# Two batches at a time, as 4x3 blocks of 256x342: 20 products in place of 2x2 blocks with 7

## The reference

```python
w = weights[conditions]                         # 128 x 128 per batch, picked by an index
x = x + einsum('bct,bcd->bdt', x, w)            # first layer, along the channels
H = einsum('btd,od->bto', x, W)                 # second layer, along the time; W is 1024 x 1024
delta = einsum('btr,bor->bto', einsum('btd,brd->btr', x, A[idx]), Bm[idx]) * scalings[idx]
x = x + H + delta                               # rank 16 adapters, picked by another index
```

## Time and profile before

| | |
|---|---|
| median of the runs | 791.12 us |
| span of the profiled execution, first to last instruction | 788.0 us |
| PE busy | 776.1 us, 98% of the span |
| PEld busy | 720.9 us |
| DVE busy | 529.8 us, 67% |
| ACT busy | 385.6 us, 49% |
| POOL busy | 120.2 us, 15% |
| DMA, mean over the span | 117 GB/s |

### The profile page before, as it was taken

How to read it: one execution, slowest core, us unless ns; L and a number is a source line. 1 busy time by engine, 2 the same in 40 slices (tenths; PEclk the granted TensorE clock), 3 DMA queues, 4 the chain that set the end, 5 groups by cost and what they waited for, 6 DMA issues and landing times.

```text
span 788.0 us, 16267 instructions
## 1 busy us (share of the span) xinstructions
PE 776.1 (98%) x5234; PEld 720.9 (91%) x5234; DVE 529.8 (67%) x942; ACT 385.6 (49%) x722; POOL 120.2 (15%) x283
## 2 busy tenths in 40 slices
PE   6999999999999999999999999999999999999998
PEld 6898999999999999999999999999999999999996
DVE  7997676666677666676666766666776567666664
ACT  6665445454444544454544455544544544545443
POOL 1021121210212101121101212012121011211000
PEclk9999999999999999999999999999999999999999
DMA  8434224333234332234231333322333322333202
GB/s 290 138 112 157 73 103 141 138 110 108 85 120 140 133 113 82 98 133 140 106 127 66 120 140 133 113 94 93 126 140 125 122 71 104 137 138 108 81 34 107
DMA packets 45335, 92.55 MB, mean 117 GB/s; under 512 B 7556, under 2 KB 23940, under 8 KB 45316
## 3 DMA queue, kind: packets, MB, share of 16 engines
q1 hardware_dynamic: 45314, 92.31, 33.5%
q10 hardware_dynamic: 2, 0.00, 0.0%
HBM read 58.72 MB, written 33.55 MB: 117 GB/s over the span
## 4 chain that ended last, share of the span: by engine, by line
PE 93%; DVE 3%; DMA 1%; SPq 1%; issue 1%; ACT 0%; DVEq 0%
PE beta L1052 34%; PE delta L1068 21%; PE alpha L1052 11%; PE beta L1065 11%; PE o_ps L1104 4%; PE o_ps L1105 4%; PE o_ps L1103 4%; PE delta L1080 2%; DMA x_odd<-wB 1%; PE alpha L1083 1%; PE beta L1083 1%; DVE wn_lo L906 1%; PE o_ps L1243 0%; DVE b_stack L893 0%; SPq L341 0%
## 5 line engine op out<-in xcount | busy, mean ns | idle before, releaser
L405 POOL TENSOR_TENSOR wr_lo<-a_ride,wr_hi 128x192 fp32r<-128x192 f32 x30 | 18.1, 603 | 561.8 <-ACT wr_hi L458 561.8
L1052 PE MATMUL beta<-wr_hi,s_hi 128*128 128x256 f32 x496 | 101.4, 286 | 2.0 <-ACT q_sb L471 1.8
L1052 PE MATMUL beta<-wr_hi,s_lo 128*128 128x256 f32 x496 | 101.1, 285 | 0.0
L1052 PE MATMUL beta<-wr_lo,s_hi 128*128 128x256 f32 x496 | 101.0, 285 | 0.0
L1068 PE MATMUL delta<-wn_hi,s_hi 128*128 128x512 f32 x244 | 97.5, 400 | 0.0
L1068 PE MATMUL delta<-wn_hi,s_lo 128*128 128x512 f32 x244 | 95.8, 393 | 0.0
L1068 PE MATMUL delta<-wn_lo,s_hi 128*128 128x512 f32 x244 | 95.3, 391 | 0.0
L880 DVE COPY o_sb<-o_ps 128x512 f32<-128x512 f32 x60 | 41.2, 687 | 76.1 <-PE o_ps L1105 76.1
L1052 PEld LDWEIGHTS beta<-wr_hi,s_hi 128*128 128x128 f32 x496 | 79.8, 188 | 5.1 <-ACT q_sb L471 2.0
L1052 PEld LDWEIGHTS beta<-wr_lo,s_hi 128*128 128x128 f32 x496 | 77.9, 188 | 0.0
L1052 PEld LDWEIGHTS beta<-wr_hi,s_lo 128*128 128x128 f32 x496 | 77.6, 188 | 0.0
(11 more groups left out here) (261 smaller groups left out, 1898.4 us busy)
## 6 DMA issues: line engine op xcount, KB each, us to landing
out<-o_sb SPq DMA_DIRECT2D x60, 512.0 KB, 2.7
x_even<-xT SPq DMA_DIRECT2D x32, 512.0 KB, 4.1
x_odd<-xT SPq DMA_DIRECT2D x30, 512.0 KB, 3.9
b_raw<-lora_b SPq DMA_DIRECT2D x192, 64.0 KB, 2.1
a_now<-lora_a SPq DMA_DIRECT2D x64, 64.0 KB, 2.4
c_raw<-cond_w SPq DMA_DIRECT2D x64, 64.0 KB, 1.8
w_raw<-wB SPq DMA_DIRECT2D x5, 512.0 KB, 6.3
x_even<-xT SPq DMA_DIRECT2D x4, 256.0 KB, 6.4
```

Source lines behind the costliest of these rows:

```text
L405: nc.gpsimd.tensor_tensor(ride_of(wr_lo, J1, J2), a_ride[:, :, 0:3, :], ride_of(wr_hi, J1, J2), ALU.subtract).then_inc(ride_ready, 1)
L1052: last = nc.tensor.matmul(bank[:, h, 0:hi - lo], left[:, chunk + k, :], right[:, k, lo:hi], start=opens and k == 0 and left is left_hi and ...
```

## The change

x of a pair is now cut in 2 x 4 blocks of 128 x 256 and the weight in 4 x 3 blocks of 256 x 342 (1026 columns, two of them zero). A block product has 2 chunks of the contraction and 3 matmuls each of 342 columns. The plain scheme has 24 products, the new one 20. Nine of them carry 16 or 32 adapter columns (358 or 374 columns wide).

```diff
-    J1, J4, J6, J2 = range(4)
-    J3, J7, J5 = range(3)
+    WITH_LEFT = ("5", "1", "3", "10", "0")
+    WITH_RIGHT = ("0", "2", "7", "11")
+    PLAIN = ("17", "15", "13", "4", "14", "18", "9", "8", "16", "19", "6", "12")
...
+            def product(o, bank, opens=False):
+                left, lo, hi = LEFT[o], BANK0[o], BANK0[o] + WIDTH[o]
+                for c in range(2):
+                    for x, w in ((x_hi, w_hi), (x_hi, w_lo), (x_lo, w_hi)):
+                        last = nc.tensor.matmul(bank[:, lo:hi], x[:, left, c * C:(c + 1) * C],
+                                                w[:, c, FIRST[o]:FIRST[o] + WIDTH[o]],
```

Six banks of PSUM hold sums (alpha, beta, pi10, pi11, pi12, pi02, with roles that alternate from pair to pair). Products are added onto sums that are still growing. Where a partial sum belongs to two results, ScalarE copies it to SBUF (c17_sb, c5_sb, c10_sb, c11_sb, c12_sb, c02_sb) or from one bank to another:

```diff
+            def seed_pi11(i, j):
+                after(act, product_done["13"], i, j, 0)
+                after(act, z_ready["01"], i, j, -1)
+                copy(main_of(bank_of(j, 0, "pi11")), main_of(bank_of(j, 0, "alpha"))).then_inc(pi11_seeded, 1)
```

The left operands are 18 blocks of 256 columns (7 of x, 11 sums), each split in high and rest, for 14 blocks' worth of columns before. The adapter has one transposed matrix for each batch (g_sb0, g_sb1). Image 1's adapter products run in the same pair; image 0's (`loras0`) after the first product of the next:

```diff
+            def loras0(i, j, d):
+                after(pe, g_ready[0], i, j, d)
+                lora("01", i, j, d)
+                after(pe, c12_half, i, j, d)
+                lora("02", i, j, d)
+                lora("00", i, j, d)
...
+                after(pe, lo_ready["u11"], i, j, 0)
+                after(pe, c_block["11"], i, j, -1)
+                multiply("17", "beta", i, j, True).then_inc(product_done["17"], 1)
+                if exists(i, j, -1):
+                    loras0(i, j, -1)
+                after(pe, lo_ready["u"], i, j, 0)
+                after(pe, ride_ready, i, j, 0, 2)
+                after(pe, c_block["10"], i, j, -1)
+                multiply("5", "alpha", i, j, True).then_inc(product_done["5"], 1)
```

All weight sums are made during the first pair, by GpSimd and VectorE, in place where blocks of W landed; ScalarE then makes each product's high part and VectorE its rest. TensorE's first pair waits for each product's weight:

```diff
+    POOL_SUMS = ("v", "s", "i21a", "i21b", "5", "e", "i11a", "i11b", "0", "4", "i32", "y", "6", "i10", "10", "i00",
+                 "7", "11", "12a", "i22", "16a", "1", "3", "19a", "12")
+    DVE_SUMS = ("f", "2", "14", "18", "11a", "9", "1a", "16", "19")
...
+            def add(name, to, x, y, op):
+                nc.gpsimd.tensor_tensor(to, x, y, op).then_inc(pool_summed, 1)
...
+            def multiply(o, role, i, j, opens=False):
+                if not exists(i, j, -1):
+                    pe.wait_ge(w_ready, SPLITS.index(o) + 1)
```

The stacks of B (high rows and rests) are no longer made for each pair by VectorE's 48 x 1024 subtraction: all of B is split once, written to a DRAM tensor, and each pair loads its stack by four DMAs, which ScalarE copies once:

```diff
-                nc.vector.tensor_tensor(b_stack[64:112, :], b_raw[64:112, :], b_stack[64:112, :], ALU.subtract)\
-                    .then_inc(b_ready, 1)
+                        sp.dma_start(b_stack_raw[row:row + 2 * R, :],
+                                     b_split[bass.ds(found[n], 1), :, :, :].rearrange("a s r o -> (a s r) o"))\
+                          .then_inc(b_landed, 16)
```

VectorE's step now has 38 instructions of 256 to 512 columns and ends so:

```diff
+                sum_c10(i, j)
+                sum_c11(i, j)
+                if exists(i, j, 1):
+                    rest_u11(i, j, 1)
+                split_xa0(i, j)
+                rest_z("10", i, j, 0)
+                rest_xa0(i, j)
+                half_c12(i, j)
+                rest_z("11", i, j, 0)
+                rest_c(i, j)
+                sum_c12(i, j)
+                if exists(i, j, 1):
+                    rest_u3(i, j, 1)
```

More of the change, by code:

```diff
@@ new lines, in upto, with after, slot_of, landed @@
+        def upto(i, j, d):
+            return i * 2 + (j + d + 1)
+        def after(eng, what, i, j, d, per=1):
+            if exists(i, j, d):
+                eng.wait_ge(what, upto(i, j, d) * per)
+        def slot_of(j, d):
+            return (j + d) % 2
+        def landed(i, j, d):
+            return (i + ((j + d) // 2 + 1)) * 16
+        def bank_of(j, d, role):
+            return banks[BANKS[(j + d) % 2][role]]
+        def main_of(bank, n=N):
+            return bank[:, R:R + n]
@@ new lines, in hi_z12, with evacuate @@
+            def hi_z12(i, j, d):
+                after(act, c_block["12"], i, j, d)
+                copy(z_hi[1][:, 2 * N:T], c12_sb[:, 0:LAST]).then_inc(z_hi_ready["12"], 1)
+            def evacuate(i, j, d, n, h):
+                after(act, o_done[n][h], i, j, d)
+                if exists(i, j, d if not n else d - 1) and not h:
+                    act.wait_ge(stored, upto(i, j, d - 1) * 32 + 16 * (1 - n))
+                copy(o_sb[:, h * H:(h + 1) * H], o_ps[h][:, :]).then_inc(o_out[n][h], 1)
@@ new lines, in plus, with rest, rest_a001, rest_a02 @@
+            def plus(to, x, y):
+                return nc.vector.tensor_tensor(to, x, y, ALU.add)
+            def rest(o, first, last, x, i, j, d):
+                after(dve, hi_ready[o], i, j, d)
+                subtract(x_lo[:, first:last, :], x, x_hi[:, first:last, :]).then_inc(lo_ready[o], 1)
+            def rest_a001(i, j, d):
+                rest("a001", A00, A02, raw(j, d)[:, 0, 0:2, :], i, j, d)
+            def rest_a02(i, j, d):
+                rest("a02", A02, A03, raw(j, d)[:, 0, 2:3, :], i, j, d)
@@ L1045, in _ @@
         def _(pe):
-            def riding(bank, left_hi, left_lo, chunk, o, rides, opens):
-                for k in range(KH):
-                    for left, right in ((left_hi, wr_hi), (left_hi, wr_lo), (left_lo, wr_hi)):
-                        for h in range(2):
-                            lo, hi = o * RS + h * Q, o * RS + (h + 1) * Q + h * rides * R
-                            last = nc.tensor.matmul(bank[:, h, 0:hi - lo], left[:, chunk + k, :], right[:, k, lo:hi],
-                                                    start=opens and k == 0 and left is left_hi and right is wr_hi,
-                                                    stop=k == KH - 1 and left is left_lo, skip_group_check=not opens)
-                return last
@@ L1229, in first_left @@
-            def first_left(k, h, bank, left_hi, left_lo, opens, o, chunk=0):
-                lo, hi = o * RS + h * Q, o * RS + (h + 1) * Q + 2 * h * R
-                for left, right in ((left_hi, wr_hi), (left_hi, wr_lo), (left_lo, wr_hi)):
-                    last = nc.tensor.matmul(bank[:, h, 0:hi - lo], left[:, chunk + k, :], right[:, k, lo:hi],
-                                            start=opens and k == 0 and left is left_hi and right is wr_hi, stop=False,
-                                            skip_group_check=True)
-                return last
```

1948 lines of the change are left out of this document (937 added, 1011 removed).

## The result

The changed kernel takes 837.6 us (median, 837.4 to 839.8), the kernel before beside it 790.9. The ratio is 1.060 (95% interval 1.0585 to 1.062): 6% slower. The forecast was 817 with a range of 788 to 834, so the direction was right and the time lies outside the range. The profiled execution has a span of 835.6 us.

The account below looks back on a forecast made before the run. TensorE's matmuls were taken to bound steady pairs, VectorE the new first pair. First pair 73.6, second 24.9, 29 pairs of 23.57 (683.5) and end 32.3 gave 814.3, plus 3.1: 817 us, range 788 to 834.

Parts of the forecast that it names:

- The 3.1 us around it: Whole kernel: added to the forecast span, because the earlier profile's span lay 3.1 us below the median of the runs.
- TensorE, per pair: Steady pair: products, conditioning, adapter matmuls and transposes sum to 22.97 us against 23.97, 1.00 us less.
- The new wait: Steady pair: TensorE waits for g_sb0 behind z12's split and VectorE's c12, 0.36 us plus 0.24 for GpSimd, 0.6 a pair.
- The port: First pair: GpSimd's SBUF reads hold up VectorE, 2.08 ns a column, bounds 0 and 26.3 us, 22.3 taken.
- Rivals 1 and 2: Whole kernel: port costs little, 779.8 to 790 us (0.23 with no change); port costs half or wait stays 0.36, 800 (0.17).
- The first pair: Start: VectorE's 45.6 us of work, start at 3.9, 1.8 of waits and 22.3 of port put the second pair at 73.6.
- The second pair: Pair after the first: pays 1.9 us of wait instead of 0.6, since VectorE reaches c12 later; 24.9 us.
- The end: Last pair and end: pair with wait, condition products, adapter matmuls, evacuation and store; 32.3 us against 31.13 before.
- Rival 3: Steady pair: VectorE sets it, through a chain longer by 0.7 us; 24.3 a pair, 838 us, chance 0.05.
- The signs named beforehand: First pairs and steady pairs: second pair's start, pair time, VectorE's busy share and an idle TensorE stretch would show the forecast.

Follow-up runs that it names:

- e1: Against the changed kernel, ScalarE copies g_sb0 (the transposed adapter rows) before it splits block z12, not behind it; 820.3 us, 1.0385 of the kernel before.
- e3: Against the changed kernel, VectorE sums block c12 before it makes the rests of z11 and c; 818.2 us, 1.0355 of the kernel before.
- f2_busy_alone: The changed kernel with only nine idle TensorE matmuls added behind the first pair, to keep its clock up; 837.7 us, 1.0602 of the kernel before.
- s1_no_pool_sums: Against the changed kernel, GpSimd's 17 weight sums cover 16 of 684 columns each, all waits kept; 821.2 us, 1.0392 of the kernel before.
- s2_sums_on_dve: Against the changed kernel, the 17 weight sums move from GpSimd to VectorE; 828.4 us, 1.048 of the kernel before.

## Why the prediction was right or wrong

Direction: right. Time: 20.6 us too low, 21.3 in the span. The 3.1 us around it were 1.3 too many (the median of before stood beside the profile of a faster execution; in each run on record the time lies 1.7 to 2.0 us above the span), and that hid a part. The steps that failed are TensorE's time of a pair, VectorE's waits in the first pair, and what follows the wait in the second. The sum's terms, in its own order:

- **TensorE, per pair: mis-sized.** Forecast 22.97, measured 23.34 without waits (e1, e3). (The terms as printed add to 22.93; and the ends of the spacing, 0.155 to 0.1585, leave 0.7 to 1.2 us of gain, not 0.75 to 1.25.) The spacing of 342 columns was right (60 product matmuls in 9.68 us; the forecast's spacings give 9.61). I left out that the product behind each transposition takes 1.00 us for 0.94, twice a pair, and that the condition block behind g_sb1 starts 0.15 late (0.38 for 0.23). With 0.07 on each 60 product matmuls these add to 0.41, the distance from 22.93. Over 29 pairs the 0.37 are 10.7 us, the largest single error. The trace of before had shown the first of these: behind its transposition at 412.59 the chain of the earlier trace rows goes on with

```profile
412.65 0.75 PE delta L1068 x3
```

and three such matmuls take 0.69 elsewhere. I built the new pair from durations alone, without a look at what follows a transposition.
- **The new wait: right in mechanism, place and size.** Forecast 0.6, measured 0.65 (1.5 us over 29 pairs). The path was forecast as 6.44 and 0.24 for GpSimd, and measures 6.68; without GpSimd it is 6.39. That the earlier trace rows bear on c's split was confirmed (0.66 for 0.42 us).
- **The port: right.** "I take 85%, 22.3" for 12,650 columns of GpSimd. The 17 sums alone cost 20.8 us, 86% of 2.08 ns a column. That 85% was a choice between 0 and 100, so its closeness is in part luck; the price itself held. Rivals 1 and 2, which let the port cost little or half, fell with it. (the earlier trace rows is no case of VectorE reading PSUM: VectorE stood idle until 415.04. The 0.47 us stay GpSimd's time undisturbed.) The Trainium skill (SBUF — State Buffer, Who interferes with whom) has a VectorE instruction with two SBUF inputs contend with a GpSimd one that reads SBUF, "not with one that only writes it". The runs agree: 9.4 us for copies, none for fills.
- **The first pair: the waits failed.** "Some 1.8 us of waits for ScalarE's halves" were 5.7, in four waits. One of 1.71 is that for the first weight block. The two of 1.76 and 2.10 had a queue behind them that I had not walked: ScalarE's weight splits stand behind partial-sum copies that wait for TensorE, and behind GpSimd sums that VectorE had held up. I had given both engines slack by their busy sums. With 0.2 more before the first instruction (4.08 for 3.9) and some 2 more of VectorE's own work and port this is the 6.2 us.
- **The second pair: 1.9 us too low.** The wait for g_sb0 was there. What I missed is what comes behind it: the adapter columns' rests on GpSimd (2.09 us), and the clock at half for the two products after them (1.2 us). Another 0.4 is the first point again. How much each would give back alone was not tested: f2_busy_alone moved the stretch at half the clock and did not remove it.
- **The end: 0.9 too low**, of which the pair's 0.4 is the first point again; the rest I did not take apart. Its terms as printed add to 32.8, not 32.3.
- **Rival 3** gave the number (838) but not the reason: its 24.3 a pair was for a chain longer by 0.7. It had 0.05. What came was the forecast's own mechanism with TensorE dearer.
- **The range: too narrow above.** The upper end of 834 left 17 us. The first two pairs (8.1) and the steady pairs (12.3) erred by more than that together, both upwards: waits and hand-overs that a sum of durations leaves out have one sign. The signs named beforehand say the same: the second pair's first product at 79.8 (70 to 78), steady pairs of 23.99 (23.3 to 23.9) and VectorE 88% busy (over 90%) all missed by a little, while the idle stretch before the adapter matmul, released by g_sb, is there.

Why the change is slower at all: with its wait taken away a pair gives 23.97 - 23.34 = 0.63 us, 19 us over 30 pairs. That would pay for a first pair longer by 19, and it is longer by 42.7. Even with 17 sums for nothing it is 24 longer (61.4 against 37.1), since VectorE is busy for 49.5 of these 61.4 us with its 20 rests, its nine sums and the operands, and waits for most of the others.

## What to carry to other kernels

A saving in the steady state must be held against what its preparation costs on the engine that bounds the start, with every reader of SBUF beside it priced; here 0.63 us a pair did not pay for it. Build a new chain from queues, not from busy sums: for each wait, name what stands ahead of the awaited instruction on its engine. Follow a wait one step further: what stands behind it may start at the lower clock. If a sum goes from VectorE to GpSimd while VectorE works in SBUF, first compare what it takes from VectorE there with its cost on VectorE.

## What the hardware showed that I had not expected

- GpSimd's sum of 684 columns takes 1.2 us from VectorE (20.8 over 17) and costs VectorE 0.78 when it makes it itself. Moving all 17 to VectorE made the kernel 9.2 us faster.
- Fills on GpSimd cost VectorE's subtractions nothing, but not every VectorE instruction: the cast of 128 columns at the start took 1.38 us beside fills in s1_no_pool_sums, and 0.23 without them.
- Small instructions can pay most: 64 columns took 1.66 us beside a weight sum and 0.22 without one (s2_sums_on_dve).
- A wait costs TensorE 0.15 us though it ends just when the matmul's turn comes. In e1_g_first the matmul before the last condition block starts at 428.12 and its follower was due 0.16 later; ScalarE's copy g_sb1 had ended at 428.27. Yet the block's first two matmuls lie 0.35 apart (428.32 and 428.67) instead of 0.23. What came late is the weight load, which otherwise starts beside the matmul before (0.35 behind the one ahead here, 0.16 else). The weight loads:

```profile
427.97 0.19 PEld L1176 LDWEIGHTS bank<-w_hi,x_lo 128*128 128x128 f32 x1
428.32 0.19 PEld L1212 LDWEIGHTS o_ps<-z_hi,c_hi 128*128 128x128 f32 x1 [0.17 <-ACT g_sb L471]
```
